# A four-layer graph network on one core: later layers' loads, wall tables and row tables issued beside other stages, and one fp32 product a tile for the rows by destination

## The chip, the cores and the metric

The kernel runs on one core of a Trainium2 chip. The metric is the time of one execution on the device in microseconds (us). Three runs of the kernel before took 7007.20, 7009.24 and 7012.14 us, with a median of 7009.24.

## What is computed

There are 3125 nodes with 128 features and 100000 edges, sorted by destination. Four residual layers follow each other, each on `relu(layernorm(x))`.

```python
h = relu(layernorm(x));  x = x + L0(h)   # three rounds of D^-1/2 A D^-1/2, summed with weights
h = relu(layernorm(x));  x = x + L1(h)   # graph attention, 8 heads of 16, an edge to itself at each node
h = relu(layernorm(x));  x = x + L2(h)   # relational convolution, 4 edge types, three rounds
h = relu(layernorm(x));  out = L3(h)     # attention over edges, with edge, node and distance terms

# L1
h = (x @ W).reshape(n, 8, 16);  a_src, a_dst = (h * att_src).sum(-1), (h * att_dst).sum(-1)
e = leaky_relu(a_src[src] + a_dst[dst], 0.2)
m = segment_max(e, dst);  ex = exp(e - m[dst]);  alpha = ex / segment_sum(ex, dst)[dst]
out = segment_sum(h[src] * alpha, dst) + bias

# L3
scores = (q[src] * k[dst]).sum(-1) / 4 + edges @ We + be
scores = scores * cons[dst] + dist_term
w = exp(scores - segment_max(scores, dst)[dst]);  weights = w / segment_sum(w, dst)[dst]
agg = segment_sum(weights * v[dst], dst)
out = layernorm(nodes + agg @ Wo + bo) * gamma + beta
```

## The kernel before

Nodes lie in W = 25 windows of P = 128, so a table of all nodes is a tile [128, 25, columns]. Edges, sorted by destination, lie in T = 816 tiles of 128 edges, none of which has destinations of two windows, and a group is G = 4 tiles: 204 groups. Most loops over groups have R = 4 places for what they load, and take 4 groups a step.

The program is a chain of blocks. In a block each engine has its own instruction list, and the engines meet at its end; within it they wait on semaphores. `vector_steps` (L1413) is the small block of the kernel: SP issues the `loads` (L1431), DVE waits for all of them and does the steps one after the other, SP waits for the last of them and issues the `stores` (L1435). `in_one_block` (L106) puts several stages into one block. A stage that is marked `own_semaphores` (L87) gives its semaphores back, and when 30 or more are spent, POOL clears them one after the other (L99) in a block of its own.

1. Set-up, sorting and counting of edges fill the first 1800 us and are not touched.
2. Layer 0: `count_product` (L1976 and on) three times. It loads the 25 blocks of counts (1600 KB each) through SP and multiplies them on PE (L2018), after ACT has scaled the first rows (L2000). Beside the third one, ahead of its products on each engine, stand `last_rows` (L1153) and `conservation` (L1185), and behind them `loc_rows` (L1457): PE turns the 816 columns of the slot numbers within their window (`k.loc`), ACT copies them, SP stores them to `k.loc_rows`.
3. Layer 1 (`layer_gat`, L2241): norm; the load of W, the attention vectors and the edge list for `PairBlocks` (L1431), whose keys DVE makes (L1578 to L1587); `project` to node rows; the scores (`l1_scores`, with the store of the rows by source); `split` (L1442), which writes the rows by destination as three bf16 parts.
4. `edge_rows` (L1593), the edge loop. For each group POOL gathers four times 128 rows by source from DRAM (L1642); SP loads the group's loc rows (L1726), each sent to all partitions; DVE compares them with the partition number (`hot_t`, L1650, bf16); PE multiplies (L1707) hot_t with the three bf16 parts of each tile's window, 12 matmuls a group, to get the rows by destination; DVE's `consume` puts them together (L2289 and L2290, or L2597 to L2611 in layer 3). In layer 1 SP also stores the gathered rows (L1730), and `PairBlocks` makes the layer-2 pair blocks beside it on PE (L1546), DVE and SP (L1569).
5. Segment maximum and sums. For these the edges are cut into CH = 16 chunks of L = 6528 slots; a chunk and one of the 8 heads make a partition, and the slot is the column. `segment_walls` (L1856) turns the destinations with `across` (L1764), so that each chunk has its 6528 destinations on 8 partitions, and writes -BIG wherever a destination differs from that of the slot ahead. `across` and `segment_max` do the same for the values. `window_sums` (L1273) then sums messages over windows, from rows that SP loads (L1297); `finish` starts with the load of `h2` and the bias (L1431).
6. Layer 2 (`layer_relational`, L2354): `read_list` (L1238), a block that loads the edge list by source and takes it apart on DVE; norm; the turning of the node rows, with the weights' load beside it; three rounds.
7. Layer 3 (`layer_attention`, L2581): norm; load of Wq, Wk, Wv, biases and others, ten in all; `project` to `qkv` of 384 columns (DVE L2626); copies of v and k into tiles of their own (L2630, L2631) and the store of q; `split` of k's rows; the ten loads of the terms by tile and two memsets (L2640, L2641); then `edge_rows`, `segment_walls`, maximum and sums, and the last norm.

## Time and profile before

| | us |
|---|---|
| median of 3 runs | 7009.24 |
| the profiled execution's own time | 7022.69 |
| its span | 7020.9 |
| PE busy | 4094.4 (58%) |
| PE weight load busy | 2368.4 (34%) |
| DVE busy | 3397.1 (48%) |
| ACT busy | 822.7 (12%) |
| POOL busy | 3466.1 (49%) |
| mean granted clock of PE | 0.729 of full speed |

The rows further down come from several views. A row of the timeline gives the start in us, the time in us, engine, line of the kernel, operation, destination <- source, shape, and, in brackets, how long the engine had been idle and what released it; "x4" stands for four instructions in a row. SPq is SP's queue: the time in its row is that of issuing. A row of the busy windows gives the window, its length, the busy time and the number of instructions of PE, PE's weight loads, DVE, ACT and POOL, then the granted clock of PE (1 is full speed), the DMA engines' mean busy share and GB/s.

### The profile page before, as it was taken

How to read it: one execution, taken by the hardware profiler on the slowest of the kernel's cores; microseconds unless marked ns; L12 is line 12 of the kernel's file. 1: busy time of each engine (PE TensorE's matmuls, PEld its weight loads, DVE VectorE, ACT ScalarE, POOL GpSimd, SP SyncE). 2: the span in 40 equal slices, each digit the busy share in tenths (PEclk: the TensorE clock that was granted, in tenths of full speed). 3: DMA queues.
4: the chain of work that ended last, by engine and by line, in shares of the span. 5: the costliest groups of instructions: out<-in, count | busy, mean ns of one | idle time of the engine just before them, and what ended most of it. 6: DMA issues, size and time to landing. Idle time of an engine off the chain costs nothing. (4 is left out here: it accounts for less than half of the span.)

```text
span 7020.9 us, 90114 instructions
## 1 busy us (share of the span) xinstructions
PE 4094.4 (58%) x17815; PEld 2368.4 (34%) x17816; DVE 3397.1 (48%) x6575; ACT 822.7 (12%) x2431; POOL 3466.1 (49%) x3349
## 2 busy tenths in 40 slices
PE   6869930015685667777724657888888633333321
PEld 5734410003332333333312543444544322222211
DVE  6866620029895255555566763122122344444465
ACT  1200000001000011221211001010010012222211
POOL 0068877755100067777702003646747437777721
PEclk6579965556797878888856988999989855555555
DMA  4311110001464467777712546666666433333310
GB/s 122 84 57 39 39 30 2 2 31 76 178 254 172 149 169 213 203 203 219 205 31 90 147 120 222 235 224 242 236 233 236 149 94 79 78 78 79 79 23 29
DMA packets 489224, 903.93 MB, mean 129 GB/s; under 512 B 96115, under 2 KB 324104, under 8 KB 449044
## 3 DMA queue, kind: packets, MB, share of 16 engines
q1 hardware_dynamic: 383278, 736.46, 31.6%
q0 software_dynamic: 105824, 165.90, 10.8%
q8 instruction: 70, 1.15, 0.1%
q14 instruction: 52, 0.43, 0.0%
HBM read 679.95 MB, written 222.12 MB: 128 GB/s over the span
## 5 line engine op out<-in xcount | busy, mean ns | idle before, releaser
L2479 POOL DMA_INDIRECT l_gathered<-l_table,l_st x816 | 777.2, 952 | 896.2 <-issue 810.2
L411 POOL DMA_INDIRECT by_src<-src_rec,src_pos x784 | 878.6, 1121 | 572.1 <-ACT attr_turned L713 333.7
L1642 POOL DMA_INDIRECT l_edges_by_src<-l_by_src,l_edges_st x816 | 793.7, 973 | 705.6 <-ACT l_edges_st L1672 457.2
L1642 POOL DMA_INDIRECT l_edges_by_src<-l_q,l_edges_st x816 | 772.2, 946 | 410.3 <-issue 243.6
L2548 PE MATMUL psum<-l_blocks,l_rows 128*128 128x512 f32 (+1 forms) x2016 | 817.2, 566 | 2.3 <-ACT l_rows L2490 2.3
L1707 PE MATMUL psum<-l_k_parts,l_edges_hot_t 128*128 x2448 | 398.4, 292 | 677.8 <-DVE l_edges_hot_t L1650 363.0
L1546 PE MATMUL psum<-pair_hot_weight,pair_hot_dst 128*128 128x512 f32 x1200 | 653.0, 687 | 219.2 <-DVE pair_hot_dst L1536 212.0
L2507 DVE TENSOR_SCALAR l_hot<-iota,l_loc,l_weight 128x128 f32<-128x128 f32 x816 | 222.3, 359 | 929.9 <-PE psum L2564 926.2
L1707 PEld LDWEIGHTS psum<-l_k_parts,l_edges_hot_t 128*128 128x128 bf16 x2448 | 254.6, 104 | 822.1 <-issue 720.1
L2548 PEld LDWEIGHTS psum<-l_blocks,l_rows 128*128 128x128 f32 x2016 | 374.5, 199 | 418.8 <-issue 414.0
L2018 PE MATMUL psum<-l_sum_counts,l_sum_rows 128*128 128x512 f32 (+1 forms) x1050 | 410.6, 554 | 129.0 <-DMA l_sum_counts<-counts 75.7
L2142 PE MATMUL psum<-near_zero 1*128 1x512 bf16 x75 | 31.6, 546 | 692.0 <-DVE near_hot L2104 688.6
L946 PE MATMUL psum<-hot_src,hot_dst 128*128 x1715 | 384.4, 374 | 25.8 <-DVE hot_dst L874 8.3
L1546 PEld LDWEIGHTS psum<-pair_hot_weight,pair_hot_dst 128*128 128x128 f32 x1200 | 239.3, 214 | 461.1 <-issue 452.7
L2564 PE MATMUL psum<-l_hot,l_gathered 128*128 128x128 f32 x1632 | 255.3, 316 | 191.3 <-issue 95.6
L1534 DVE TENSOR_SCALAR pair_hot_weight<-pair_iota,pair_staged 128x512 f32<-128x512 f32 x600 | 331.8, 553 | 20.6 <-PE psum L1546 20.5
L2597 DVE TENSOR_TENSOR l_edges_by_src<-l_edges_by_src,psum 128x512 f32<-128x512 f32 x204 | 140.2, 687 | 415.0 <-DMA l_edges_by_src<-l_q,l_edges_st 407.2
L2564 PEld LDWEIGHTS psum<-l_hot,l_gathered 128*128 128x128 f32 x1632 | 234.8, 223 | 228.6 <-issue 228.2
L1331 PE MATMUL psum<-l_sum_rows,l_sum_hot 128*128 128x128 f32 x1632 | 239.1, 291 | 124.7 <-issue 123.7
L2018 PEld LDWEIGHTS psum<-l_sum_counts,l_sum_rows 128*128 128x128 f32 x1050 | 190.6, 193 | 348.9 <-issue 272.9
L872 DVE TENSOR_SCALAR hot_src<-count_iota,tile_shifted 128x3200 f16 x245 | 259.5, 1059 | 73.0 <-PE psum L946 52.9
L2087 DVE MEMSET near_zero<- 1x256 uint32 x1 | 0.3, 272 | 580.1 <-PEq L95 580.1
(471 smaller groups left out, 5850.2 us busy)
## 6 DMA issues: line engine op xcount, KB each, us to landing
l_blocks<-pair_blocks SPq DMA_DIRECT2D x216, 1024.0 KB
l_sum_counts<-counts SPq DMA_DIRECT2D x75, 1600.0 KB, 8.0
pair_blocks<-pair_block SPq DMA_DIRECT2D x25, 3072.0 KB
l_edges_loc<-loc_by_tile SPq DMA_DIRECT2D x416, 128.0 KB, 3.1
l_rows<-l_edges_by_src SPq DMA_DIRECT2D x204, 256.0 KB
l_sum_rows<-l_rows SPq DMA_DIRECT2D x204, 256.0 KB, 2.6
attr_then_counts<-in_edge_attr SPq DMA_DIRECT2D x14, 1568.0 KB
counts<-attr_then_counts SPq DMA_DIRECT2D x13, 1600.0 KB, 7.3
```

Of the source, the lines that this page charges most:

```text
L411: pool.indirect_dma_start(table, bass.IndirectOffsetOnAxis(ap=pos[:, e:e + 1], axis=0), rec[:, e, :], None).then_inc(s_out[g % R], 16)
L872: v.tensor_scalar(hot_src[:, bass.ds(place, 1), 0:NP].rearrange("p a c -> p (a c)"), iota[:, :], shifted[:, 0, bass.ds(t, 1)], None, ALU.i ...
L946: ins = pe.matmul(k.ps[c][:, 0:m], hot_dst[:, bass.ds(place, 1), :].rearrange("p a c -> p (a c)"), hot_src[:, bass.ds(place, 1), col:col + ...
L1331: ins = pe.matmul(k.psum[:, bass.ds(to[g] * D, D)], hot[:, r, g, :], rows[:, r, g, :], start=False, stop=False)
L1534: v.tensor_scalar(self.hot_w[:, place, :], self.wide[:, :], self.near[:, q, j, 1:2], self.near[:, q, j, 2:3], ALU.is_equal, ALU.mult).then ...
L1546: pe.matmul(self.bank(b), self.hot_d[:, place, :], self.hot_w[:, place, :], start=j == self.first[b], stop=j + 1 == self.first[b + 1]).the ...
L1642: pool.indirect_dma_start(a[:, r, g, :], None, table_src, bass.IndirectOffsetOnAxis(ap=st[:, r, g:g + 1], axis=0))\
L1707: ins = pe.matmul(by_place[:, q, g, 0:cols_dst], hot_t[:, r, g, :], by_dst[:, bass.ds(of[g], 1), j, :].rearrange("p a c -> p (a c)"), star ...
L2018: ins = pe.matmul(k.ps[b][:, 0:n], st[:, u, :], cnt[:, u, col:col + n], start=w == 0, stop=w == W - 1)
L2479: pool.indirect_dma_start(sent[:, p, g, :], None, by_type, bass.IndirectOffsetOnAxis(ap=st[:, p, g:g + 1], axis=0))\
L2548: ins = pe.matmul(k.ps[c][:, 0:n * P].rearrange("p (a s) -> p a s", s=P), rows[:, b, t * D:(t + 1) * D], blocks[:, 0:n, t, :], start=b == ...
L2564: ins = pe.matmul(k.psum[:, bass.ds(to[g] * P, P)], sent[:, p, g, :], hot[:, p, g, :], start=False, stop=False)
```

## The change

The loads that stood in blocks of their own go beside other work: `layernorm` gets a list of loads that SP issues while the norm runs, and its block ends when they have landed. W, attention vectors and edge list of layer 1, the edge list and weights of layer 2, and weights and terms of layer 3 go there. DVE's steps on these (`pair_keys`, now in `l1_scores`, and `list_steps`, now in the turning of layer 2) follow in later blocks. `h2` and the bias of layer 1 are loaded ahead of the last six steps of `window_sums`.

`split` is gone. The rows by destination stay fp32, hot_t is fp32, and a tile takes one product instead of three. Layer 3 writes v and k straight to one tile `rows` from the projection, in two adds a window; q has a tile of its own.

`segment_walls` is gone. `slot_rows` writes the destinations and the walls by slot to DRAM once, beside the third count product (its first part ahead of `last_rows`, its stores behind the product's loads), and each `edge_rows` loads them in its last eight groups, 16 loads of 8 partitions and two small ones. `segment_max` gets two memsets and two copies for the ends.

```diff
-def layernorm(k, tag, src, dst, relu=True, gamma=None, beta=None):
+def layernorm(k, tag, src, dst, relu=True, gamma=None, beta=None, loads=()):
...
+            if loads:
+                @block.sync
+                def _(sp):
+                    for to, what in loads:
+                        sp.dma_start(to, what).then_inc(s_ld, 16)
+                    sp.wait_ge(s_ld, 16 * len(loads))
...
         def sync(sp):
+            late = 6
+            for first, behind in ((0, steps - late), (steps - late, steps)):
+                if first > 0:
+                    for to, what in loads:
+                        sp.dma_start(to, what).then_inc(s_ld, 16)
+                with sp.Fori(first, behind) as i:
...
-def loc_rows(k, ctx):
+def slot_rows(k, ctx):
...
     def tensor(pe):
+        pe.wait_ge(s_set, 3)
+        for bank, table in ((0, k.loc[:, 0:T]), (2, k.dst_f[:, 1:T + 1])):
+            for c in range(C7):
+                ins = pe.transpose(block(bank, c, wide(c)), table[:, c * P:c * P + wide(c)], k.ident[:, :])
             ins.then_inc(s_tr, 1)
+        for c in range(C7):
+            ins = pe.matmul(k.ps[4][0:wide(c), c:c + 1], k.dst_f[:, c * P:c * P + wide(c)], k.ident[:, P - 1:P],
+                            start=True, stop=True)
+        ins.then_inc(s_tr, 1)
+        pe.wait_ge(s_kept, 2 * C7)
+        pe.wait_ge(s_wall, 1)
...
+        v.tensor_tensor(wall[:, :, 1:P], dst[:, :, 1:P], dst[:, :, 0:P - 1], ALU.not_equal).then_inc(s_wall, 1)
+        v.tensor_tensor(wall[:, :, 0:1], dst[:, :, 0:1], last[:, :].unsqueeze(2), ALU.not_equal).then_inc(s_wall, 1)
+        v.wait_ge(s_wall, 3)
+        v.tensor_scalar(wall[:, :, :], wall[:, :, :], -BIG, None, ALU.mult).then_inc(s_wall, 1)
...
+        for to, what in ((k.loc_rows, turned), (k.dst_rows, dst), (k.wall_rows, wall)):
+            sp.dma_start(to[0:whole * P, :].rearrange("(c q) e -> q c e", q=P), what[:, 0:whole, :]).then_inc(s_st, 16)
+            sp.dma_start(to[whole * P:T, :], what[0:T - whole * P, whole, :]).then_inc(s_st, 16)
...
-        hot_t = k.sb(ctx, f"{tag}_hot_t", [P, R, G, P], BF16)
+        hot_t = k.sb(ctx, f"{tag}_hot_t", [P, R, G, P])
...
-                    for j in range(3):
-                        ins = pe.matmul(by_place[:, q, g, 0:cols_dst], hot_t[:, r, g, :],
-                                        by_dst[:, bass.ds(of[g], 1), j, :].rearrange("p a c -> p (a c)"),
-                                        start=j == 0, stop=j == 2)
+                    ins = pe.matmul(by_place[:, q, g, 0:cols_dst], hot_t[:, r, g, :],
+                                    by_dst[:, bass.ds(of[g], 1), :].rearrange("p a c -> p (a c)"),
+                                    start=True, stop=True)
...
-                for i in range(W // 2 * 2 * per + 1, steps):
+                late = W // 2 * 2 * per + 1
+                for i in range(late, steps):
                     for r in range(R):
+                        seg.load(sp, s_seg, (i - late) * R + r, (steps - late) * R)
                         group(i * R + r, r, i)
...
+    def load(self, sp, sem, n, of):
+
+        flat = lambda table: table.rearrange("(c t) e -> c (t e)", c=CH)
+        for c in range(n * CH // of, (n + 1) * CH // of):
+            sp.dma_start(self.wall[c * HEADS:(c + 1) * HEADS, 0:L], flat(self.k.wall_rows)[c, :].partition_broadcast(HEADS))\
+                .then_inc(sem, 16)
...
-                    count_product(k, f"l0_sum{r}", scaled, acc, [last_rows(k, beside), conservation(k, io, beside)], [loc_rows(k, beside)])
+                    turned, stored = slot_rows(k, beside)
+                    count_product(k, f"l0_sum{r}", scaled, acc,
+                                  [turned, last_rows(k, beside), conservation(k, io, beside)], [stored])
...
-            split(k, "l1_dst", by_dst, dst_parts)
...
-                segment_walls(k, "l1_walls", seg)
...
+                    def keep(v, n, ps):
+                        v.tensor_tensor(q[:, n, :], ps[:, 2 * D:3 * D], b[:, 2 * D:3 * D], ALU.add)
+                        return v.tensor_tensor(rows[:, n, 0:2 * D], ps[:, 0:2 * D], b[:, 0:2 * D], ALU.add)
```

Three places show how instructions stand. First DVE's list where the block of the third count product begins. Before:

```order
L2235 TENSOR_TENSOR l_scaled<-l_h,dinv 128x3200
L1418 UNCONDITIONAL_BRANCH
L115 UNCONDITIONAL_BRANCH
L1164 COPY last_tmp<-psum 128x25
L1165 SCALAR_TENSOR_TENSOR last_tmp<-ones,last_tmp 128x25
```

With the change:

```order
L2234 TENSOR_TENSOR l_scaled<-l_h,dinv 128x3200
L1416 UNCONDITIONAL_BRANCH
L115 UNCONDITIONAL_BRANCH
L1475 MEMSET loc_beyond 16x128
L1476 MEMSET dst_turned 128x128
L1477 MEMSET dst_tile_behind 128x1
L1481 COPY dst_tile_behind<-psum 128x1 x6
L1481 COPY dst_tile_behind<-psum 48x1
L1485 TENSOR_TENSOR walls_turned<-dst_turned 128x7x127
L1486 TENSOR_TENSOR walls_turned<-dst_turned,dst_tile_behind 128x7
L1488 TENSOR_SCALAR walls_turned<-walls_turned 128x896
L1172 COPY last_tmp<-psum 128x25
```

The nine steps of `slot_rows` now stand ahead of `last_rows`, whose first step is L1164 before and L1172 with the change. Second, SP's list at the end of layer 1's edge loop, the last groups. Before:

```order
L1726 DMA l_edges_loc<-loc_by_tile 128x512
L1730 DMA l_rows<-l_edges_by_src 512x1x128
L1726 DMA l_edges_loc<-loc_by_tile 128x512
L1730 DMA l_rows<-l_edges_by_src 512x1x128
L1569 DMA pair_blocks<-pair_block 128x12x512
L109 UNCONDITIONAL_BRANCH
L1428 UNCONDITIONAL_BRANCH
```

With the change (L1852 loads walls, L1857 the two rows of ends):

```order
L1726 DMA l_edges_loc<-loc_by_tile 128x512
L1730 DMA l_rows<-l_edges_by_src 512x1x128
L1852 DMA l_segments_wall<-wall_by_tile 8x6528 x2
L1726 DMA l_edges_loc<-loc_by_tile 128x512
L1730 DMA l_rows<-l_edges_by_src 512x1x128
L1852 DMA l_segments_wall<-wall_by_tile 8x6528 x2
L1857 DMA l_segments_ends<-dst_by_tile 1x16x1 x2
L1726 DMA l_edges_loc<-loc_by_tile 128x512
L1730 DMA l_rows<-l_edges_by_src 512x1x128
L1570 DMA pair_blocks<-pair_block 128x12x512
L109 UNCONDITIONAL_BRANCH
```

Two wall loads stand ahead of each of the last eight groups' loc load and row store, and all of them ahead of the last store of the pair blocks. Third, SP's list at the head of layer 3, from the last two of the ten weight loads. Before, with the branches that end and begin blocks:

```order
L1431 DMA l_vecs<-in_L_gnn_gamma 128x128
L1431 DMA l_vecs<-in_L_gnn_beta 128x128
L1418 UNCONDITIONAL_BRANCH
L1428 UNCONDITIONAL_BRANCH
L1435 DMA l_q<-l_qkv 128x25x128
L1418 UNCONDITIONAL_BRANCH
L1428 UNCONDITIONAL_BRANCH x2
L1431 DMA l_terms_by_tile<-attr_terms 128x6x128 x8
L1431 DMA l_terms_by_tile<-attr_terms 128x8x16
L1431 DMA l_terms_by_tile<-dist_terms 128x8x784
L1418 UNCONDITIONAL_BRANCH
```

With the change:

```order
L211 DMA l_vecs<-in_L_gnn_gamma 128x128
L211 DMA l_vecs<-in_L_gnn_beta 128x128
L211 DMA l_terms_by_tile<-attr_terms 128x6x128 x8
L211 DMA l_terms_by_tile<-attr_terms 128x8x16
L211 DMA l_terms_by_tile<-dist_terms 128x8x784
L185 UNCONDITIONAL_BRANCH
L1426 UNCONDITIONAL_BRANCH
L1433 DMA l_q<-l_q_rows 128x25x128
L1416 UNCONDITIONAL_BRANCH
L115 UNCONDITIONAL_BRANCH
```

The loads of the terms have moved from behind q's store into the norm's block, straight behind the weights.

## Rows read from the trace of the kernel before

**Rows 1.** Busy windows: the edge loop of layer 1, its end, the loop of layer 3

```profile
2480.00:3532.00 1052.00, 805.71 (x3648) 390.58 (x3648) 542.30 (x1815) 212.69 (x528) 793.74 (x816) 0.84 0.73 202
...
3486.00:3542.00 56.00, 21.33 (x108) 11.06 (x108) 12.17 (x46) 6.33 (x16) 27.93 (x30) 0.66 0.88 211
...
5702.00:6732.00 1030.00, 398.42 (x2448) 254.57 (x2448) 467.15 (x1226) 217.58 (x1023) 772.17 (x816) 0.50 0.34 78
```

**Rows 2.** Groups of POOL: busy us, mean ns | idle before, releasers

```profile
L1642 POOL DMA_INDIRECT l_edges_by_src<-l_by_src,l_edges_st x816 | 793.7, 973 | 705.6 <-ACT l_edges_st L1672 457.2 <-issue 232.0 <-ACT l_edges_st L1685 13.7
...
L1642 POOL DMA_INDIRECT l_edges_by_src<-l_q,l_edges_st x816 | 772.2, 946 | 410.3 <-issue 243.6 <-ACT l_edges_st L1672 161.7 <-ACT l_edges_st L1685 4.9
```

**Rows 3.** Timeline: start and end of count product 3

```profile
2240.57 2.05 PE L2018 MATMUL psum<-l_sum_counts,l_sum_rows 128*128 128x512 f32 x2 [53.31 <-ACT l_sum_rows L2000]
...
2380.46 2.07 DVE L2008 COPY l_acc<-psum 128x512 f32<-128x512 f32 x4
...
2389.77 3.49 DVE L2231 TENSOR_TENSOR l_acc<-l_acc,dinv 128x3200 f32<-128x3200 f32 x1 [6.99 <-PEq L95]
```

**Rows 4.** Timeline: head of layer 1

```profile
2433.05 1.01 DVE L1578 TENSOR_SCALAR pair_iota<-iota 128x128 f32<-128x128 f32 x4 [11.84 <-DMA pair_edges<-by_src]
...
2475.93 0.57 DVE L1449 CAST l_dst_parts<-l_dst_rows 128x400 bf16<-128x400 f32 x1 [8.10 <-PEq L1418]
...
2479.41 0.38 ACT L1672 COPY l_edges_st<-src_i 128x4 int32<-128x4 int32 x3 [28.12 <-PEq L1418]
```

**Rows 5.** Timeline: end of layer 1's edge loop

```profile
3531.46 0.19 DVE L2289 COPY l_own<-psum 128x32 f32<-128x32 f32 x1 [6.16 <-DMA l_edges_by_src<-l_by_src,l_edges_st]
...
3544.80 6.96 DVE L2298 SCALAR_TENSOR_TENSOR l_shares<-l_shares 128x6528 f32<-128x6528 f32 x1 [13.06 <-PEq L95]
```

**Rows 6.** Timeline: the walls stage of layer 1, first step, and first step behind it

```profile
3559.55 0.92 ACT L1793 COPY l_walls_dst_st<-dst_f 128x384 f32 x2 [35.11 <-PEq L1803]
...
3588.70 0.92 ACT L1793 COPY l_val_st<-l_top 128x384 f32 x2 [14.85 <-PEq L1803]
```

**Rows 7.** Timeline: between the sums and the finish of layer 1

```profile
4181.60 0.39 SPq L1431 DMA_DIRECT2D l_h_back<-l_by_src  x1
...
4188.96 0.77 DVE L2339 TENSOR_TENSOR l_sums<-l_sums,some_edge 128x200 f32<-128x200 f32 x2 [21.27 <-DMA l_bias<-in_L_gnn_bias]
```

**Rows 8.** Timeline: head of layer 2

```profile
4216.77 0.07 DVE L1256 MEMSET l_index<- 128x16 int32 x1 [7.18 <-DMA read_src_buf<-by_src]
```

**Rows 9.** Timeline: head of layer 3, from the norm to the first gather

```profile
5594.82 3.49 DVE L189 TENSOR_REDUCE ln_stat<-x_sb 128x25 f32<-128x3200 f32 x1 [6.74 <-PEq L95]
...
5619.82 0.43 SPq L1431 DMA_DIRECT2D l_vecs<-in_L_gnn_beta  x1
...
5624.33 1.94 PE L1386 MATMUL psum<-ident,l_h 128*128 128x128 f32 x8 [39.66 <-PEq L1418]
...
5646.16 3.49 DVE L2630 COPY l_v<-l_qkv 128x3200 f32<-128x3200 f32 x1 [0.53 <-PEq L109]
...
5659.56 3.69 DVE L1449 CAST l_k_parts<-l_k_rows 128x3400 bf16<-128x3400 f32 x1 [7.56 <-PEq L1418]
...
5678.65 9.46 SPq L1431 DMA_DIRECT2D l_terms_by_tile<-attr_terms  x9
...
5700.29 0.38 DVE L2640 MEMSET l_terms_by_tile<- 128x384 f32 x1 [22.11 <-DMA l_terms_by_tile<-dist_terms]
...
5702.78 0.95 POOL L1642 DMA_INDIRECT l_edges_by_src<-l_q,l_edges_st  x1 [161.75 <-ACT l_edges_st L1672]
```

**Rows 10.** Timeline: eight fp32 matmuls of the window sums

```profile
4001.24 1.15 PE L1331 MATMUL psum<-l_sum_rows,l_sum_hot 128*128 128x128 f32 x8 [0.53 <-issue]
```

**Rows 11.** Groups of instructions by shape, DVE in layer 2

```profile
L2515 DVE TENSOR_SCALAR l_update<-l_update,l_bias 128x512 f32<-128x512 f32 x18 | 8.7, 486 | 0.6
```

**Rows 12.** DMA issues: count, KB each, median us from issue to landing

```profile
own_by_slot<-l_own SPq DMA_DIRECT2D x1, 3264.0 KB, 9.1
```

**Rows 13.** Waits of SP's queue: us in all, times, longest

```profile
SPq L142 <- DMA x_sb<-in_x: 4.7, 1, 4.7
```

More of the change, by code:

```diff
@@ L1278, in window_sums @@
+@own_semaphores
+def window_sums(k, tag, stream, shares, own_rows, sum_rows, own, sums, loads=()):
     steps = T // (R * G)
@@ L1463, in loc_rows @@
     beyond = k.sb(ctx, "loc_beyond", [R * G, P], BF16)
-    s_tr, s_kept, s_set, s_st = (k.sem(f"loc_{name}") for name in ("turned", "kept", "beyond_set", "stored"))
+    dst = k.sb(ctx, "dst_turned", [P, C7, P])
+    last = k.sb(ctx, "dst_tile_behind", [P, C7])
+    wall = k.sb(ctx, "walls_turned", [P, C7, P])
+    s_tr, s_kept, s_set, s_wall, s_st = (k.sem(f"slots_{name}") for name in ("turned", "kept", "set", "walls", "stored"))
     per = PSUM_BANK // P
-    halves = [range(c, min(c + per, C7)) for c in range(0, C7, per)]
@@ L1500 @@
+    return {"tensor": tensor, "scalar": scalar, "vector": vector}, {"sync": sync}
 class PairBlocks:
@@ L1732, in sync @@
             if pairs is None:
-                with sp.Fori(0, steps) as i:
+                late = 2
+                with sp.Fori(0, steps - late) as i:
                     for r in range(R):
                         group(i * R + r, r, i)
+                for n in range(late * R):
+                    seg.load(sp, s_seg, n, late * R)
+                    group((steps - late) * R + n, n % R, steps - late + n // R)
             else:
@@ L2269, in scores @@
             def scores(v, step):
+                pair_keys(v, step, k, edge, pair_iota, ctx)
                 for q, dst in ((0, by_src[:, :, D:D + HEADS]), (1, by_dst[:, :, 0:HEADS])):
```

288 lines of the change are left out of this document (119 added, 169 removed).

## The prediction

> **What bounds the kernel now.** I read the busy windows first, to see which engine sets each edge loop, then the instruction groups, then the timeline at each stage boundary that the change touches. 0.2% (14 us) is about what a measurement can tell from no change.
>
> The first edge loop (layer 1) runs 1052 us for 204 groups, 5.16 each; POOL is busy 793.7, PE 805.7 at a mean granted clock of 0.84, DVE 542.3 [rows 1]. POOL's gathers take 973 ns each with a constant issue gap of 232 us in all [rows 2], and 793.7 + 232 is nearly the whole loop: POOL bounds it. So does it in layer 3: 772.2 + 243.6 of 1030 us, PE busy only 398.4 although its clock is 0.50. In both, work of DVE, PE, ACT and SP is covered as long as it fits in about 5.1 us a group. Everything between the loops is a chain of blocks, in which each duration counts in full, and so does each load that a block waits for. The reader should look there for the gain.
>
> **Part by part.**
>
> *Tables by slot, ahead of the third count product.* Before, PE idles 53.3 us until the first row is scaled, because DVE and ACT work through last_rows and conservation [rows 3]. The new stage stands ahead of these and nothing covers it. PE: 14 transposes and 7 one-column fp32 products of two records each, 28 records; eight transposes take 1.94 us [rows 9], so 0.24 each, 6.8. DVE: seven small copies, then the wall steps over 896 columns, by 3.49 us for 3200 columns [rows 3] about 1.0, 0.2 and 0.5; ACT's copies overlap PE. With overlap between them I take **+9** (bounds +5 and +14). At the product's end, the DVE idles from 2382.53 to 2389.77 [rows 3], 7.2 us, for the turning of loc, its stores and the 38 clears. Clears cost 6.74 us for 88 [rows 9], 0.077 each, so 3.1 remains: **-4.1**. The seven stores now go out behind the count loads, and the product's last 10 us cover them.
>
> *Head of layer 1.* DVE idles 11.84 us for pair_edges [rows 4]; 2.5 of it is the clears, 9.3 the loads, now issued beside a norm of some 20 us, and a block boundary (0.53, the idle before L2630 [rows 9]) goes too: **-9.8**. pair_keys' steps are moved, not removed. The split from 2475.93 to ACT's first step at 2479.41 [rows 4] goes: **-3.5**.
>
> *The fp32 product in the loops.* Twelve bf16 matmuls a group become four fp32 ones, eight records. Nearest row: eight fp32 records of 128 columns take 1.15 us at nearly full clock [rows 10], so at most 1.37 at 0.84 and 2.3 at 0.50. Below, nothing excludes a gain, since layer 3's twelve take 1.95 at 0.50 (398.4/204). Even +0.8 us for each of 204 groups is 163 of 246 idle us of PE. The fp32 selector costs DVE 0.49 us (128x512 f32 [rows 11]) where it now has half its time free. Covered by POOL: **0** in both loops (bounds -5 and +26, rival C).
>
> *Port.* A longer fp32 step on DVE could hold up the gathers. Layer 1's gathers take 27 ns more than layer 3's [rows 2], with more such DVE work beside them; so 0.12 us more a group is worth about 1 us a loop. I leave it at 0. At the other bound each of these 0.12 us stops the gathers: 25 us a loop, 6949 in all, which is a small rival below. The Trainium skill ("SBUF — State Buffer", "Who interferes with whom") states such a lock: a DVE `tensor_scalar` in a two-port mode shuts GpSimd out for the whole instruction. The two loops of the trace, 27 ns a gather apart, speak for the small figure.
>
> *Wall loads in the last eight groups.* 16 loads of 8 partitions x 6528 floats, 3264 KB. The same bytes over 128 partitions land in 9.1 us [rows 12]. In layer 1 the queues are 0.88 busy over the last 56 us [rows 1], 6.7 us free. On all queues it is 9.1 - 6.7 = +2. Should loads of 8 partitions reach only half of them, it is 18.2 - 6.7 = +11.5. DVE's last step is at 3531.46 and the leaky step starts at 3544.80, behind the stores [rows 5]. I take **+12**, nearer to the narrow kind of load, since these are narrow. Layer 3's queues are 0.34 busy, so 8 groups of 5.05 leave 27 us free: **+2** for landing behind the last group (bounds 0 and rival B's figure).
>
> *The walls stage.* 3559.55 to 3588.70 [rows 6], 29.15 us; one in each of two layers. Two memsets and two copies come back inside segment_max, 0.8 us. **-28.3 twice, -56.6**.
>
> *Sums and finish of layer 1.* The load wait of 4181.60 to 4188.96 [rows 7] goes, -7.4, but 1664 KB now stand ahead of the row loads of the last six steps, in a loop with four places of slack: +5.5 (bounds 0 and 7.4). **-1.9**.
>
> *Head of layer 2.* DVE's idle of 7.18 us for the list [rows 8] goes; the list's steps move to behind the turning and stay serial. The weights were hidden and stay so. **-7.2**.
>
> *Head of layer 3.* Norm to first gather: 5594.82 to 5702.78, 108.0 [rows 9]. After: SP issues 20 loads from 5594.8 on, ten at 0.47 each as now (4.7; the tenth is issued at 5619.82), nine in 9.5, then 12.2 until the last has landed (5688.1 to 5700.29): 5621.2, so the norm of some 20 us does not quite cover them and its block ends 6 us late. Boundary 0.5; transposes to rows as before, 5624.33 to 5646.16, 21.8; three small steps 1.3; the store's 7.56 stays; 1.6 to POOL. First gather at 5654, **-48.8**. What goes is the split (19.1), the terms' wait (22), two copies (5646.16 to the store at 5652.0, of which 0.4 stays) and boundaries. Project now has two adds a window on DVE, 0.2 us longer; PE's products (384 columns) set its pace.
>
> *Clears.* 252 become 242: **-0.8**.
>
> Sum: +9 - 4.1 - 9.8 - 3.5 + 12 + 2 - 56.6 - 1.9 - 7.2 - 48.8 - 0.8 = **-109.7**. The profiled execution took 7022.69 us (span 7020.9), so its like would take 6913; it stands 13.5 above the median of the runs shown, 7009.24, against which the forecast is **6899**.
>
> **Rivals.**
>
> *B: the narrow loads hold up both loops' ends.* The only narrow load in this trace, x's last 26.5 KB, kept SP waiting 4.7 us alone [rows 13]. If sixteen come one after the other, that is 75 us from the first's issue, eight groups ahead of the end: 3486.7 + 75 = 3562 instead of 3541.5 in layer 1 (+20), 6692 + 75 = 6767 instead of 6734 in layer 3 (+33). Against the 12 and 2 taken, +39: **6938**. For it: layer 1's queues are full. Against: the queues work in parallel, and a load of 204 KB is not 26 KB from a cold start. The Trainium skill ("DMA: Bandwidth & Descriptors", "Why a DMA increments its semaphore by 16 and not by 1") has a load from SP spread over the largest count up to 16 that divides its outer dimension: 8 of 16 engines here, always the lowest. By that rule the eight engines carry everything and the range reaches to B. The trace does not show an eight-partition load.
>
> *C: PE becomes a second bound in layer 1.* A mean clock of 0.84 means about a third of the loop at 0.50, some 65 groups; 2.3 against 1.95 there is +0.4 a group where PE already has no slack: +26, **6925**. Against: these products have 16 columns, not 128.
>
> *D: slower.* PE's granted clock falls to 0.50 for the whole first loop, because the work on it comes in other lumps. PE then needs 805.7 x 0.84/0.50 = 1354 us instead of 1052: +302, **7200**. It turns the sign once PE needs 5.16 + 0.54 = 5.7 us a group, a mean clock of 0.58. For it: layer 3's loop is at 0.50 throughout, with PE 0.39 busy. Against: PE is busy 0.77 of this loop, and the fp32 pair products that make up most of that stay.
>
> *E: the moved loads hide nothing.* Should load and norm slow each other or the blocks wait as long as before, 9.3 + 7.2 + 4.7 and the terms' 22 come back: +43, **6942**. Against: the norm's steps touch no queue, and SP issues nothing else then.
>
> **How the numbers follow.** Forecast (its own range 6883 to 6915) 0.60; B 0.18; C 0.08; E 0.04; DVE holding up the gathers 0.04 (to 6949); no loss at tails nor at the tables (below 6883) 0.03; D 0.03. The range 6880 to 6942 leaves out D, most of the port case and the ends. Faster 0.95, within 0.2% 0.02 (several of the losses together), slower 0.03.
>
> **What would show it.** In the new profile: ACT's val step right behind the leaky step, no L1793 on dst_f; the first gather of layer 3 some 59 us behind the norm's start; one group of fp32 products under 1.4 us at full clock; gathers still 950 to 975 ns with the 0.30 gap; DVE's leaky step 24 to 26 us behind its last loop step (13.3 before), less if the loads spread well. The forecast is wrong if the loops themselves get longer (gathers over 1 us, PE's clock under 0.7), or if a loop's end waits over 30 us on the walls.

## The result, and the profile after

The changed kernel takes 6917.5 us (median of four runs, 6906.7 to 6927.9) against 7008.2 us before, a ratio of 0.9865 (0.9853 to 0.9877): 91 us faster. The forecast was 6899 with a range of 6880 to 6942. The page of the changed kernel begins:

```profile
span 6918.8 us, 82626 instructions
...
PE 4075.5 (59%) x15832; PEld 2543.6 (37%) x16095; DVE 3407.3 (49%) x6559; ACT 802.6 (12%) x2404; POOL 3451.8 (50%) x3349
```

The profiled execution is 102 us shorter than that of before. Two stretches that the change does not touch account for 12 of these: 3.9 up to the end of the scaling ahead of the third count product, and 8.6 in layer 2's rounds (1263.5 us before, 1255.0 after; a second profile of the kernel before gave 1245.3). The rest is 90, as the medians say. Stage by stage, from one profile of each kernel, with the forecast's terms:

| stretch, us | before | after | difference | forecast |
|---|---|---|---|---|
| scaling to the third product's start | 54.9 | 61.6 | +6.8 | +9 |
| the third product's last copy to DVE's next step | 7.2 | 3.8 | -3.5 | -4.1 |
| layer 1: norm's end to first gather | 59.3 | 46.4 | -12.9 | -13.3 |
| layer 1: first to last gather | 1041.3 | 1055.2 | +13.9 | 0 |
| layer 1: last gather to leaky step | 23.0 | 38.4 | +15.4 | +12 |
| leaky step to `across` of the values, and the four new steps behind it | 43.9 | 15.5 | -28.4 | -28.3 |
| window sums and the wait for the finish | 381.7 | 380.5 | -1.2 | -1.9 |
| layer 1's end to layer 2's first product | 74.8 | 67.3 | -7.5 | -7.2 |
| start of layer 2's last run of products to layer 3's first gather | 154.9 | 109.0 | -45.8 | -48.8 |
| layer 3: first gather to last score | 1029.6 | 1033.2 | +3.5 | +2 |
| last score to `across` of the values | 33.9 | 1.2 | -32.8 | -28.3 |
| from there to the end | 254.6 | 257.0 | +2.4 | in the row above, and the clears |

The rows add up to -90.1, against -109.7 in the forecast; 17.3 of the 19.6 between them lie in the two rows on layer 1's loop and its end.

The busy windows of the changed kernel, over layer 1's loop, its end, and layer 3's loop (columns as in [rows 1]):

```profile
2467.00:3523.00 1056.00, 804.27 (x2824) 451.07 (x2824) 578.39 (x1806) 208.20 (x525) 788.41 (x816) 0.83 0.74 203
...
3485.00:3560.00 75.00, 21.79 (x66) 13.31 (x66) 10.74 (x39) 5.55 (x14) 17.06 (x18) 0.57 0.70 142
...
5627.00:6661.00 1034.00, 443.26 (x1632) 379.32 (x1632) 499.09 (x1227) 217.50 (x1020) 772.65 (x816) 0.50 0.35 81
```

The first loop has PE at 0.83 instead of 0.84, and its mean DMA share hardly moved. At its end the difference stands: in [rows 1] the last 56 us moved 211 GB/s at a share of 0.88, here the last 75 us move 142 GB/s at 0.70. The groups of POOL, beside [rows 2]:

```profile
L1643 POOL DMA_INDIRECT l_edges_by_src<-l_by_src,l_edges_st x816 | 788.6, 966 | 714.9 <-ACT l_edges_st L1673 447.4 <-issue 229.2 <-DMA l_rows<-l_edges_by_src 23.3
...
L1643 POOL DMA_INDIRECT l_edges_by_src<-l_q,l_edges_st x816 | 772.7, 947 | 366.4 <-issue 238.9 <-ACT l_edges_st L1673 116.4 <-ACT l_edges_st L1686 11.1
```

The gathers did not get slower (966 and 947 ns against 973 and 946). What grew is POOL's wait for the store of the gathered rows: 23.3 us, where it was 2.7 before. The timeline at the third product ([rows 3]) and at the head of layer 1 ([rows 4]):

```profile
2243.51 2.90 PE L2015 MATMUL psum<-l_sum_counts,l_sum_rows 128*128 128x512 f32 x3 [54.42 <-ACT l_sum_rows L1997]
...
2383.39 2.08 DVE L2005 COPY l_acc<-psum 128x512 f32<-128x512 f32 x4
...
2389.24 3.49 DVE L2230 TENSOR_TENSOR l_acc<-l_acc,dinv 128x3200 f32<-128x3200 f32 x1 [3.78 <-PEq L95]
...
2423.76 1.94 PE L1384 MATMUL psum<-ident,l_ln 128*128 128x128 f32 x8 [39.66 <-PEq L95]
...
2435.61 1.01 DVE L1579 TENSOR_SCALAR pair_iota<-iota 128x128 f32<-128x128 f32 x4 [0.54 <-PEq L109]
```

DVE's step on the product's result waits 3.78 us instead of 6.99. In layer 1, PE starts 3 us behind the norm's end, where it had to wait for loads and `pair_keys`; these steps now stand behind the projection, at 2435.61, with a boundary's idle of 0.54. The end of layer 1's loop ([rows 5]) and what follows ([rows 6]):

```profile
3542.82 0.18 DVE L2287 TENSOR_TENSOR l_shares<-l_edges_by_src,psum 128x32 f32<-128x32 f32 x1
...
3560.67 6.96 DVE L2296 SCALAR_TENSOR_TENSOR l_shares<-l_shares 128x6528 f32<-128x6528 f32 x1 [17.67 <-PEq L95]
...
3575.43 0.92 ACT L1797 COPY l_val_st<-l_top 128x384 f32 x2 [39.32 <-PEq L1807]
```

From DVE's last step to the leaky step it is 17.7 us of idle instead of 13.1. ACT's first step of `across` stands directly behind DVE's two steps: no walls stage. The end of the sums and the head of layer 2 ([rows 7, 8]):

```profile
4162.67 8.95 PE L1333 MATMUL psum<-l_sum_zero 1*128 1x512 f32 x14
...
4175.55 0.77 DVE L2338 TENSOR_TENSOR l_sums<-l_sums,some_edge 128x200 f32<-128x200 f32 x2 [16.18 <-PEq L95]
...
4196.66 0.34 SPq L211 DMA_DIRECT2D l_list<-by_src  x1
...
4217.65 1.73 PE L2397 MATMUL psum<-ident,l_rows 128*128 128x128 f32 x7 [46.02 <-PEq L185]
```

DVE's first step of the finish comes 3.9 us behind the products' end, 4 us sooner than before, and PE's turning starts 21.0 us behind the norm's start: the loads (issued from 4196.66 on) are covered. The head of layer 3 ([rows 9]):

```profile
5565.44 3.49 DVE L189 TENSOR_REDUCE ln_stat<-x_sb 128x25 f32<-128x3200 f32 x1 [5.98 <-PEq L95]
...
5570.04 11.87 SPq L211 DMA_DIRECT2D l_terms_by_tile<-attr_terms  x9
...
5581.95 1.73 SPq L211 DMA_DIRECT2D l_terms_by_tile<-dist_terms  x1
...
5594.56 1.94 PE L1384 MATMUL psum<-ident,l_h 128*128 128x128 f32 x8 [38.51 <-PEq L185]
...
5617.44 0.39 DVE L2635 COPY l_rows<-conservation 128x200 f32<-128x200 f32 x1 [0.53 <-PEq L109]
...
5627.51 0.94 POOL L1643 DMA_INDIRECT l_edges_by_src<-l_q,l_edges_st  x1 [116.38 <-ACT l_edges_st L1673]
```

Norm's start to first gather is 62.1 us instead of 108.0; 59 were forecast. The terms' nine loads take 11.87 us to issue beside the norm, where they took 9.46 alone, and the block's end is that much later.

**Where layer 1's gain went.** SP's queue in the changed kernel, in the last eight groups of the loop:

```profile
3479.44 1.78 SPq L1852 DMA_DIRECT2D l_segments_wall<-wall_by_tile  x2
...
3481.32 0.36 SPq L1726 DMA_DIRECT2D l_edges_loc<-loc_by_tile  x1
...
3489.72 0.56 SPq L1730 DMA_DIRECT2D l_rows<-l_edges_by_src  x1
...
3526.84 0.96 SPq L1852 DMA_DIRECT2D l_segments_wall<-wall_by_tile  x2
...
3535.57 0.57 SPq L1570 DMA_DIRECT2D pair_blocks<-pair_block  x1
```

The load of loc rows at 3481.32 is issued behind two wall loads. DVE's selector, which compares these rows, waits for it:

```profile
3490.82 0.49 DVE L1651 TENSOR_SCALAR l_edges_hot_t<-l_edges_loc,pid 128x512 f32<-128x512 bf16 x1 [11.70 <-issue]
...
3499.65 0.48 DVE L1651 TENSOR_SCALAR l_edges_hot_t<-l_edges_loc,pid 128x512 f32<-128x512 bf16 x1 [6.20 <-issue]
```

In the last groups DVE idles 53.1 us ahead of seven selectors, where it idled 5.6 ahead of two before. (The profile names "issue" as the releaser; in the kernel the selector waits for the loc load alone.) 9.5 us lie between issue and use at 3490.82, where such a load lands in 3.1 in the median of the kernel before. The row store that follows DVE's work, at 3489.72, comes 8.4 us behind the loc load's issue, and that repeats group after group.

The last pair store is issued at 3535.57, 1068.5 us behind the loop's first gather; before it was 1051.5 (at 3532.07). That is 17 of the 29 us lost here. The other 12.5 are this store's own: its last packet ends 21.9 us behind its issue, where it took 9.4 before. The walls' last packet ends at 3548.5, the pair store's at 3557.5. So what the block's end waits for is the pair store, which has wall loads beside it for its first 13 us.

POOL meanwhile waits for the row stores, since they free the place that it gathers into:

```profile
3494.30 0.94 POOL L1643 DMA_INDIRECT l_edges_by_src<-l_by_src,l_edges_st  x1 [7.11 <-DMA l_rows<-l_edges_by_src]
...
3510.82 0.96 POOL L1643 DMA_INDIRECT l_edges_by_src<-l_by_src,l_edges_st  x1 [4.81 <-DMA l_rows<-l_edges_by_src]
```

Two windows of 20 us there, before and after:

```profile
3490.00:3510.00 20.00, 11.42 (x49) 5.43 (x49) 8.51 (x30) 3.94 (x10) 15.19 (x16) 0.74 0.87 259
...
3510.00:3530.00 20.00, 6.40 (x50) 4.08 (x48) 1.92 (x9) 1.81 (x6) 9.72 (x11) 0.62 0.89 81
```

```profile
3490.00:3510.00 20.00, 11.71 (x29) 6.31 (x30) 7.04 (x24) 3.12 (x7) 7.61 (x8) 0.67 0.75 144
...
3510.00:3530.00 20.00, 10.08 (x38) 7.00 (x36) 2.25 (x11) 2.24 (x6) 7.56 (x8) 0.59 0.80 121
```

Before, the first of them moves 259 GB/s at a share of 0.87, after the change 144 at 0.75, and POOL issues 8 gathers instead of 16. The DMA engines look busy and move little. The trace of the packets says why: the 128 packets of wall loads, 26112 bytes each, took 2.7 us apiece in the loop. A loc load stands behind two wall loads on the same queue; two such packets ahead of it on an engine are 5.5 us (an estimate from these numbers), near the 6.4 by which it came later.

### The profile page after: what moved, and what is told of

Its sections match the earlier page's. It is cut to its first block and busy times, and to the rows that moved or that the text cites. A ratio compares the mean times of both kernels' runs of the same rounds, so it can differ in the third digit from the quotient of the medians.

```text
span 6918.8 us, 82626 instructions
## 1 busy us (share of the span) xinstructions
PE 4075.5 (59%) x15832; PEld 2543.6 (37%) x16095; DVE 3407.3 (49%) x6559; ACT 802.6 (12%) x2404; POOL 3451.8 (50%) x3349
## 5 line engine op out<-in xcount | busy, mean ns | idle before, releaser
L1707 PE MATMUL psum<-l_rows,l_edges_hot_t 128*128 x1632 | 443.3, 453 | 596.2 <-DVE l_scores L2609 579.4
L1707 PEld LDWEIGHTS psum<-l_rows,l_edges_hot_t 128*128 128x128 f32 x1632 | 379.3, 330 | 660.4 <-issue 660.4
L953 PE MATMUL psum<-hot_src,hot_dst 128*128 x1470 | 342.3, 370 | 65.7 <-issue 52.6
L1651 DVE TENSOR_SCALAR l_edges_hot_t<-l_edges_loc,pid 128x512 f32<-128x512 bf16 x414 | 211.8, 512 | 307.1 <-DMA l_edges_loc<-loc_by_tile 183.2
```

The source lines that it names most:

```text
L953: ins = pe.matmul(k.ps[c][:, 0:m], hot_dst[:, bass.ds(place, 1), :].rearrange("p a c -> p (a c)"), hot_src[:, bass.ds(place, 1), col:col + ...
L1707: ins = pe.matmul(by_place[:, q, g, 0:cols_dst], hot_t[:, r, g, :], by_dst[:, bass.ds(of[g], 1), :].rearrange("p a c -> p (a c)"), start=T ...
```

## The experiments

Chips differ here. The kernel before took 8223 us on the chip of the first four experiments, 7010 on that of the next four, 8205 on that of the last four, so runs are compared within their group. On the slower chips POOL's gathers take 983 ns, little more than elsewhere, but the loops are about 1315 and 1280 us long: POOL waits 250 to 290 us in each for the row numbers that ACT stages. Beside the ratios I use three stretches of layer 1 that stand in every profile: first to last gather, last gather to leaky step, leaky step to `across`.

### The walls' part undone

```diff
-                        seg.load(sp, s_seg, (i - late) * R + r, (steps - late) * R)
...
+                segment_walls(k, "l1_walls", seg)
...
+                segment_walls(k, "l3_walls", seg)
...
-                                  [turned, last_rows(k, beside), conservation(k, io, beside)], [stored])
+                    count_product(k, f"l0_sum{r}", scaled, acc, [last_rows(k, beside), conservation(k, io, beside)], [loc_rows(k, beside)])
```

> The changed kernel with the walls stage back in both layers, no wall loads in the loops and the slot table reduced to loc behind the third count product, as before the change. By the two traces, the walls stage is worth 29.1 us in layer 1 and some 29 to 32 in layer 3, against it stand 13.9 us in layer 1's loop, 15.4 at its end, 3.5 at layer 3's end and 3.3 at the third count product. Theory (the loads give back all of layer 1's gain): 26 us slower than the changed kernel, ratio to before about 0.990, and layer 1's loop from first to last gather 1041 us instead of 1055. Rival (the loop got longer for another reason, as the fp32 products): the loop stays at 1055 and the whole is 40 us slower, ratio 0.992.

Measured: ratio 0.9788 (0.9774 to 0.9801), 8050 us. The chip being of the slower kind, the ratio can't be laid beside 0.9865. The stretches are 1314.7, 21.0 and 41.5 us.

### Wide loads, and layer 1's loads beside the leaky step

Narrow is what the changed kernel does: 16 loads of 8 partitions x 6528 columns. Wide is the same bytes in 8 loads of 128 partitions x 816 columns.

```diff
-        for c in range(n * CH // of, (n + 1) * CH // of):
-            sp.dma_start(self.wall[c * HEADS:(c + 1) * HEADS, 0:L], flat(self.k.wall_rows)[c, :].partition_broadcast(HEADS))\
-                .then_inc(sem, 16)
+        cols = slice(n * L // of, (n + 1) * L // of)
+        sp.dma_start(self.wall[:, cols], flat(self.k.wall_rows)[:, cols].unsqueeze(1).to_broadcast([CH, HEADS, L // of]))\
+            .then_inc(sem, 16)
```

> The changed kernel, but each of the last eight groups loads 816 columns of the walls for all 128 partitions in one transfer, instead of two transfers of 6528 columns for 8 partitions. Same bytes, same place. Theory (narrow loads: 8 partitions keep few queues busy for long, so the loc loads and row stores behind them land late): layer 1's cost of 29 us falls to 5 to 12, 20 us faster than the changed kernel, ratio about 0.984. Rival (volume: 3.3 MB more in a stretch whose queues are full, in whatever shape): no change, ratio 0.9865, loop and end as in the changed kernel.

```diff
-                        seg.load(sp, s_seg, (i - late) * R + r, (steps - late) * R)
...
-                vector_steps(k, "l1_leaky", leaky)
+                def walls(sp):
+                    for n in range(2 * R):
+                        seg.load(sp, s_lw, n, 2 * R)
+                    sp.wait_ge(s_lw, 16 * Segments.LOADS)
+                in_one_block(k, {"vector": lambda v: leaky(v, Chain(v, s_lv)), "sync": walls})
```

> The changed kernel, but layer 1's wall loads (narrow, as they are) are issued in the block of the leaky step, 13.9 us of DVE work, not in the edge loop. Layer 3 as changed. Loop and end of layer 1 go back to 1041 and 23 us (-29). Theory (narrow loads use about half the queues): they take some 20 us from issue to the last landing, 6 to 10 longer than the leaky step: net 20 faster than the changed kernel, ratio 0.984. Rival (volume alone, 9 to 10 us): hidden, net 29 faster, ratio 0.982. If loads go one after the other (4.7 each), 75 us: 32 slower than the changed kernel.

The fourth kernel has both edits.

> Both edits: wide loads, layer 1's in the block of the leaky step, layer 3's in the last eight groups. Theory and rival both: hidden under 13.9 us of DVE work, layer 1's whole cost of 29 us gone, and up to 3 more in layer 3: 29 to 32 faster than the changed kernel, ratio 0.982. Should wide loads still take over 14 us, the leaky block ends later by the difference.

| kernel, same chip | us | ratio | first to last gather | to leaky step | to `across` |
|---|---|---|---|---|---|
| walls' part undone | 8050 | 0.9788 | 1314.7 | 21.0 | 41.5 |
| wide, in the loop | 8010 | 0.9740 | 1323.8 | 23.4 | 14.8 |
| narrow, beside leaky | 8057 | 0.9798 | 1322.1 | 23.8 | 56.8 |
| wide, beside leaky | 8011 | 0.9741 | 1314.4 | 20.5 | 15.8 |

The loop's own length scatters here by some 5 us either way: of the three kernels without loads in it, rows 1, 3 and 4, it took 1314 to 1322, and its end 20.5 to 23.8. So wide loads in the loop cost at most 9 in it and 3 at its end, and perhaps nothing. The third row speaks clearest. There nothing else uses the queues, and the 16 narrow loads hold the block for 56.8 us, 42 more than the leaky step alone. SP's row and busy windows of that kernel, from the leaky step on:

```profile
4227.42 5.70 SPq L1852 DMA_DIRECT2D l_segments_wall<-wall_by_tile  x16
```

```profile
4227.00:4241.00 14.00, 0.00 (x0) 0.00 (x0) 13.50 (x2) 0.00 (x0) 0.00 (x0) 0.50 0.48 60
...
4241.00:4260.00 19.00, 0.00 (x0) 0.00 (x0) 0.42 (x1) 0.00 (x0) 0.00 (x0) 0.50 0.54 66
```

The same of the fourth kernel, with eight wide loads:

```profile
4215.73 5.19 SPq L1852 DMA_DIRECT2D l_segments_wall<-wall_by_tile  x8
```

```profile
4216.00:4231.00 15.00, 0.00 (x0) 0.00 (x0) 13.69 (x2) 0.00 (x0) 0.00 (x0) 0.50 0.82 223
```

Issuing takes about as long (5.70 and 5.19 us). But the narrow loads keep the share at 0.48 to 0.54 and move 60 to 66 GB/s, while the wide ones reach 0.82 and 223 GB/s.
### The changed kernel and the kernel before, on one chip

> The changed kernel, unaltered, beside the others of this group, since chips differ (the kernel before takes 7008 us on one and 8223 us on another). On the faster kind of chip: ratio 0.9865. On the slower kind, where runs without the walls' part stood at 0.9788 and with wide loads at 0.974: ratio 0.978 to 0.982, and layer 1's loop 10 to 15 us longer than the 1314 of the run without wall loads, if the narrow loads are what costs.

> The kernel before, for its profile on this chip. Ratio 1. If the three bf16 products a tile cost nothing in the loops (as forecast), both edge loops are as long as with one fp32 product: on the faster kind 1041 and 1020 us, on the slower kind 1314 and 1281. If they cost time there, its loops are longer by 20 to 100 us on the slower kind, which would account for the 173 us between it and the run without the walls' part, of which the stages outside the loops explain only some 75.

The chip was of the faster kind: 6926.6 us against 7009.6, ratio 0.9879 (0.9864 to 0.9895); the kernel before against itself 1.0005. The stretches repeat: 1043.6, 24.3, 43.9 before and 1054.5, 38.4, 14.8 with the change. The narrow loads' cost in layer 1 is 25 us by this pair, 29 by the first.

### Three bf16 parts again

The walls' part is undone here too, and hot_t is bf16 again, so in its loops this kernel does what the kernel before did.

```diff
+            split(k, "l1_dst", by_dst, dst_parts)
...
+                split(k, "l3_k", krow, k_parts)
...
-                    ins = pe.matmul(by_place[:, q, g, 0:cols_dst], hot_t[:, r, g, :],
-                                    by_dst[:, bass.ds(of[g], 1), :].rearrange("p a c -> p (a c)"),
-                                    start=True, stop=True)
+                    for j in range(3):
+                        ins = pe.matmul(by_place[:, q, g, 0:cols_dst], hot_t[:, r, g, :],
+                                        by_dst[:, bass.ds(of[g], 1), j, :].rearrange("p a c -> p (a c)"),
+                                        start=j == 0, stop=j == 2)
```

> The kernel of the first experiment (no walls' part) with split back in both layers: the rows by destination in three bf16 parts, twelve bf16 matmuls a group, hot_t in bf16. Forecast's view (the loops are bound elsewhere): only the splits come back, 3.5 + 19 = 22.5 us, so some 48 us slower than the changed kernel on the faster kind of chip (ratio 0.993 to 0.994) and 22 slower than the first experiment on either kind. Rival (the products cost time in the loops): 20 to 100 us more than that on the slower kind, in the loops' length.

Measured: 6957.7 us, ratio 0.9925 (0.9911 to 0.9938), 31 slower than the changed kernel beside it and not 48. Of the missing 17, layer 2's rounds, which no edit touches, gave 10 in the profiled pair (1247.2 against 1257.2). The stages are as expected: 3.3 us at the head of layer 1, 17.0 at that of layer 3 for the splits. The loops are 1040.5 and 1018.2 us, as those of the kernel before (1043.6 and 1017.7). Their counterpart with one fp32 product and no narrow loads in layer 1's loop is the kernel of the next section: 1037.5 and 1019.9 us, and 23.9 from last gather to leaky step against 24.7 here. So the fp32 product costs nothing in either loop, and does not stretch the first one's end. POOL, DVE and PE in layer 1's loop with three parts:

```profile
L1639 POOL DMA_INDIRECT l_edges_by_src<-l_by_src,l_edges_st x816 | 793.1, 972 | 695.4 <-ACT l_edges_st L1669 447.0 <-issue 229.8 <-ACT l_edges_st L1682 14.6
...
L1647 DVE TENSOR_SCALAR l_edges_hot_t<-l_edges_loc,pid 128x512 bf16<-128x512 bf16 x414 | 154.9, 374 | 210.5 <-DMA l_edges_loc<-loc_by_tile 170.4 <-issue 35.8 <-PE psum L1704 0.3
...
L1704 PE MATMUL psum<-l_dst_parts,l_edges_hot_t 128*128 x2448 | 194.3, 174 | 50.5 <-DVE l_edges_hot_t L1647 38.6 <-issue 5.3 <-DVE l_shares L2309 2.0
```

The same of the changed kernel on that chip:

```profile
L1643 POOL DMA_INDIRECT l_edges_by_src<-l_by_src,l_edges_st x816 | 788.8, 967 | 713.6 <-ACT l_edges_st L1673 447.0 <-issue 226.3 <-DMA l_rows<-l_edges_by_src 22.2
...
L1651 DVE TENSOR_SCALAR l_edges_hot_t<-l_edges_loc,pid 128x512 f32<-128x512 bf16 x414 | 212.1, 513 | 299.1 <-DMA l_edges_loc<-loc_by_tile 179.5 <-issue 117.5
...
L1707 PE MATMUL psum<-l_dst_rows,l_edges_hot_t 128*128 x1632 | 203.5, 257 | 48.8 <-DVE l_edges_hot_t L1651 35.4 <-DVE l_shares L2287 9.5 <-issue 3.9
```

The fp32 products cost PE 9 us over the whole loop, and the fp32 selector costs DVE 57 us, of 1040 in which both have room. The gathers beside the longer DVE step take 967 ns in the mean, not more than the 972 beside the shorter one. Those 196 that had a selector beside them for over 100 ns took 995 ns, the others 958 (961 and 975 with bf16), so a small hold-up can't be excluded, but it does not show in the loop's length.

### Wide loads beside the leaky step, and the slot tables behind last_rows

```diff
-                    count_product(k, f"l0_sum{r}", scaled, acc,
-                                  [turned, last_rows(k, beside), conservation(k, io, beside)], [stored])
+                    cleared, conserved = conservation(k, io, beside)
+                    count_product(k, f"l0_sum{r}", scaled, acc,
+                                  [cleared, last_rows(k, beside), turned, conserved], [stored])
```

> Wide wall loads, layer 1's beside the leaky step, and the slot tables' steps behind last_rows on each engine, with conservation's memset ahead of both, so that its loads fly meanwhile. Against the wide loads beside the leaky step alone: the 6.8 us that the slot tables cost ahead of the third product go, and DVE starts on conservation some 3 us earlier than before the change, as its load wait of 6.3 us is filled: 7 to 10 faster. In all 36 to 42 faster than the changed kernel, ratio 0.981 on the faster kind, 0.973 on the slower.

Measured: 6884.0 us, ratio 0.9820 (0.9806 to 0.9833), 42.6 faster than the changed kernel beside it. It beats both kernels. This is the removal of layer 1's narrow loads on a faster chip. Layer 1 reads 1037.5, 23.9 and 17.0 us, and the stretch from scaling to the norm's end 232.2 instead of 238.6: layer 1 gives 29 of the 43 us, the slot tables' new place 6.5. Three rows of its timeline, on SP and DVE, show how:

```profile
2190.65 0.33 SPq L1215 DMA_DIRECT2D cons_wc<-in_L_gnn_Wc  x1
...
2194.66 0.17 DVE L1477 MEMSET loc_beyond<- 16x128 bf16 x1
...
2202.04 0.99 DVE L1224 TENSOR_TENSOR cons_hidden<-cons_node_vec,cons_wc 128x800 f32<-128x800 f32 x1
```

SP issues conservation's first load at 2190.65, ahead of the tables' steps, which begin on DVE at 2194.66. At 2202.04 DVE goes on with conservation without a wait.

### A second chip of the slower kind

> Wide loads in the last eight groups of both loops again, to be read against the changed kernel on a chip of the faster kind (ratio 0.9865 and 0.9879 there). There the changed kernel's layer 1 takes 1055 us from first to last gather and 38 from there to the leaky step, 29 more than before. Theory (narrowness costs, not volume): 1040 to 1046 and 23 to 32; 15 to 22 faster than the changed kernel, ratio 0.984 to 0.985. Rival (volume): 1055 and 38, no change.

> Layer 1's walls beside the leaky step in one transfer of 128 partitions x 6528 columns: rows of 26 KB as in the narrow loads, all partitions as in the wide ones. From the leaky step's start to across: 56.8 us with narrow loads, 15.8 with eight wide ones of 3.3 KB rows. If the count of partitions in a transfer is what costs: 15 to 18 us. If long rows cost: 40 to 57 us.

> The changed kernel, only with the slot tables' steps behind last_rows and conservation's memset first. From the end of the scaling on DVE to the norm's end in layer 0: 238.8 us in the changed kernel, 232.2 in the combined one, 235.5 before the change. Expected 232.2, and the whole 6.6 faster than the changed kernel, ratio 0.9860 to 0.9865: within what a measurement tells of it, so the place in the profile decides. A rival: the six loads now compete with the counts' loads and DVE waits longer for them: 235 or more.

> No walls' part again, on the faster kind of chip. By the stages of the two profiles there, the walls' part as a whole gains 25 us: 26.7 in layer 3, 1.4 in layer 1 (29.1 less 27.7 lost at the loop), minus 3.3 at the slot tables. So 25 slower than the changed kernel, ratio 0.990 to 0.9915, layer 1's loop 1041 and 24 to the leaky step. Rival (the fp32 product is what stretched the loop's end): 1055 and 38 stay.

The edits are as above; the one wide load is `seg.load(sp, s_lw, 0, 1)`, layer 1's walls in a single transfer. The chip was again of the slower kind, so what was expected of ratios on the faster one stays untested, and the group is read in itself:

| kernel, same chip | us | ratio | first to last gather | to leaky step | to `across` |
|---|---|---|---|---|---|
| narrow in the loop (slots behind) | 8012 | 0.9768 | 1316.1 | 33.9 | 14.8 |
| wide in the loop | 7990 | 0.9740 | 1311.8 | 22.0 | 14.8 |
| one wide load beside leaky | 7998 | one run | 1318.2 | 19.2 | 19.4 |
| no walls' part | 8043 | 0.9804 | 1307.7 | 19.5 | 41.8 |

Wide instead of narrow loads, at the same place, is 21 us here, although the first row has the slot tables' gain. Up to the leaky step, narrow loads add 22.8 us to the last row's loop without loads (1350.0 against 1327.2) and wide ones 6.6, but the third row, without loads too, has 1337.4, so these sums are good to 10 us.

The last pair store scatters far less. From its issue to the end of its last packet it takes 9.4 to 10.1 us in every profile without narrow loads in the loop, those with wide loads in it included (10.0 and 9.9), and 21.9, 22.1 and 20.2 in the three with narrow ones, of which the last is the first row here. Volume as the cause falls.

One transfer with rows of 26 KB holds the block for 19.4 us where 15 to 18 were expected, not far from the 15.8 of eight transfers with 3.3 KB rows and far from 56.8: it is mostly the number of partitions in a transfer that costs, and the row's length 4 us at most. POOL's own wait for row stores is only 4.7 us with narrow loads on this chip. The slot tables' place gives 4 us here (234.6 against 238.5) and 6.5 on the faster chip. Without the walls' part the kernel is 31 us slower than the first row, which itself has these 4; 25 were expected against the changed kernel.

## Why the prediction was right, and where it was off

The time lay in the range and the sign was clear. By the medians the gain was 91, the forecast 110.

**Right, term by term.** The heads of layers 1 and 2 came to -12.9 and -7.5 (forecast -13.3, -7.2), the walls stage to -28.4 in layer 1. In layer 3 it came to -32.8, since clears of semaphores that stood ahead of the stage moved behind it; 2.4 came back there, net -30 (-34 in the second pair of profiles). The slot tables cost 6.8 and gave back 3.5 (forecast 9 and 4.1): 28 records on PE took 4.9 us, not 6.8. The fp32 products cost nothing in either loop, as the experiment with three parts shows beside the combined kernel; that had been chosen at 0 between -5 and +26. The gathers beside the longer DVE step were 967 ns against 972, so the port term's other bound, 25 us a loop, did not come about. Rival C, that PE becomes a second bound, fails by the same rows, and rival D by the clock: 0.83 in the loop.

**The term that was mis-sized** is "wall loads in the last eight groups", +12 in layer 1. Loop and end together measured +29 (25 in the second pair). My bound took half of the engines at full rate, 18.2 us for the bytes. Alone, the narrow loads hold a block for 56.8 us: 3.5 us for each of 16, near the 4.7 of the one narrow load in the trace of before [rows 13], which I had kept for rival B.

The place was wrong too. I had the block's end wait for the walls' own landing, with DVE's leaky step 24 to 26 us behind its last loop step. It came 17.9 us behind it, against 13.2 before, and the walls had landed 9 us ahead of the pair store. The loss lay in the loop's own transfers. The step that failed is "work of DVE, PE, ACT and SP is covered as long as it fits in about 5.1 us a group": the loads' issue fits, but what stands behind them on the queue does not. Places are freed by row stores, which SP issues only when a group is done, and a group needs its loc load, which now stands behind wall loads. So POOL itself waited, 23.3 us in all, and the last pair store was issued 17 us later and took 12.5 longer. That 12.5 lies near the +12 taken is luck: it is another transfer's time.

Rival B, the narrow loads one after the other, came nearer to the mechanism. It priced the end of layer 1's loop at +20 against the measured 29; in layer 3 it had +33 and the loop's end measured +3.5 (+7.7 in the second pair), with the DMA engines at a share of 0.35. The result lies between the forecast and B.

**The smaller miss** is the head of layer 3, -45.8 against -48.8. SP's issue of the terms' loads takes 2.4 us longer beside the norm than alone, and it stands on the path there, since the norm is shorter than the loads. Rival E, that moved loads hide nothing, was wrong but for this.

**The base.** The sum was set against a median. The profiled execution of before lay 14.5 us above the median of 7008.2, that of after 3.4, so the pair's 102 flatters the change by 11; layer 2's rounds alone scatter by 18 us between two profiles of one kernel.

**Open.** On the slower chips the kernel without the walls' part is 162 and 173 us ahead of the kernel before, on the faster one the stages give some 70 for the same parts. No profile of the kernel before exists there, so which part gains the rest isn't known; three bf16 parts against one fp32 product on such a chip was not tried. Wide loads inside the loop were not run on a faster chip, nor the changed kernel itself on a slower one. Nor was it tried why a packet of a narrow load takes 3.3 us, against 2.0 for one of the same size in the single wide load: a port, or eight engines reading one row of DRAM at a time, are both open.

## What to carry to other kernels

A transfer moved beside a busy loop must be judged by how many partitions it spans, not by its bytes: 16 loads of 8 partitions cost 25 to 29 us on the faster chips and some 13 to 23 on a slower one; the same bytes in 8 loads of 128 partitions cost 12 at most on the slower chips. And a DMA put into a loop's queue stands ahead of the loop's own loads and stores; look for the wait behind it (here a store that frees a gather's place) even if the engine that bounds the loop touches none of it. A stage that leaves the queue free is no cure by itself: beside the leaky step narrow loads held the block 42 us longer, more than they cost in the loop, and wide ones came out the same in either place (8011 and 8010 us). The loads that a norm of 21 us covered, at the heads of layers 1 and 2, gave about what was forecast of them.

## What was not expected of the hardware

- Loads of 8 partitions of 26 KB moved 60 GB/s at a DMA share of 0.48, eight packets at a time of 3.3 us each; loads of all 128 partitions moved 223 at 0.82 (both alone with DVE's leaky step).
- A store of 3 MB behind narrow loads took 20 to 22 us, and 9.4 to 10.1 without them, beside wide loads too.
- Two chips differ by 17% on this kernel (7010 against 8223 us) while POOL's gathers differ by 1%: the first edge loop is 1041 us on one and, in kernels without wall loads in it, 1308 to 1322 on the slower chips.
- The same stretch of layer 2 took 1245 to 1264 us over six profiles on the faster chips, with no edit in it.
